# Four stacked attention layers on one core: maxima added to the scores by one product per tile and round, and another sequence of pieces in the second attention

## The reference

```python
# layer 0: 16 heads
x = ln(x + mha(x, x, causal=True));  x = ln(x + mha(x, ctx));  x = ln(x + ffn_gelu(x))
# layer 1: 4 heads
x = x + mha(x, x); x = x + swiglu(x); x = x + mha(x, ctx); x = x + swiglu(x)
# layer 2: 8 heads, beside it a recurrence over the 100 rows
h_t = (1 - gate) * h_prev + gate * z_t + g_t * h_prev     # gate = sigmoid(... + h_prev @ Wgh)
x = x + h_seq + mha(q, ctx) + 0.1 * v;  x = x + ffn_gelu(rms(x))
# layer 3
a = softmax(x @ ctx.T);  x = tanh(concat(x, a @ ctx) @ W + b) + x
```

## Time and profile before

| | |
|---|---|
| median of 3 runs | 1629.91 us (1627.28 to 1635.43) |
| the profiled execution | 1633.46 us, span 1631.7 us |
| TensorE busy | 1569.6 us, 96% |
| VectorE busy | 766.9 us, 47% |
| ScalarE busy | 670.7 us, 41% |
| mean granted TensorE clock | 0.969 |
| products with maxima (L530) | 1152, mean 236 ns |
| score products (L533), in passes | 2304, means 299 and 343 ns |

### The profile page before, as it was taken

The page is one execution under the profiler, slowest core; times in us unless marked ns, Lnnn a source line. Parts: engine busy times, 40 slices in busy tenths (PEclk is TensorE's granted clock), DMA queues, the critical chain, the costliest instruction groups (busy, mean ns, idle before and its releaser), DMA issues.

```text
span 1631.7 us, 30754 instructions
## 1 busy us (share of the span) xinstructions
PE 1569.6 (96%) x13256; PEld 1026.5 (63%) x13256; DVE 766.9 (47%) x1568; ACT 670.7 (41%) x1417; POOL 252.2 (15%) x442
## 2 busy tenths in 40 slices
PE   8899899999999999999999999999899999999997
PEld 7555566666665556555677765554677767665565
DVE  1577657667642256211233332226565567562132
ACT  2455456646554433111333422125453444343343
POOL 1333300100000000000122210000243344320000
PEclk9999999999999999999999999999798799899999
DMA  4311000000000010000100000000000000020031
GB/s 154 99 50 43 12 27 2 1 2 1 2 27 0 0 78 1 20 1 0 78 1 1 1 11 16 0 7 1 27 2 2 2 2 2 2 77 0 0 93 58
DMA packets 19560, 36.97 MB, mean 23 GB/s; under 512 B 2048, under 2 KB 17376, under 8 KB 18272
## 3 DMA queue, kind: packets, MB, share of 16 engines
q1 hardware_dynamic: 19424, 35.01, 6.5%
HBM read 33.36 MB, written 1.64 MB: 21 GB/s over the span
## 4 chain that ended last, share of the span: by engine, by line
PE 87%; DVE 7%; ACT 4%; issue 1%; DMA 1%; POOL 0%; SPq 0%; DVEq 0%; ACTq 0%
PE psum L420 38%; PE psum L755 11%; PE psum L533 9%; PE psum L465 8%; PE psum L571 6%; PE psum L503 3%; PE psum L860 2%; PE psum L530 2%; DVE maxima L1387 2%; PE psum L888 1%; PE psum L901 1%; PE psum L853 1%; PE psum L869 1%; ACT probs L1063 1%; PE psum L566 1%
## 5 line engine op out<-in xcount | busy, mean ns | idle before, releaser
L420 PE MATMUL psum<-x_resid,weights 128*128 128x400 f32 x832 | 294.5, 504 | 4.3 <-ACT probs L1063 1.6
L1387 DVE TENSOR_REDUCE maxima<-psum 100x2 f32<-100x722 f32 (+3 forms) x332 | 243.5, 758 | 113.7 <-PE psum L503 96.1
L420 PEld LDWEIGHTS psum<-x_resid,weights 128*128 128x128 f32 x832 | 156.1, 191 | 121.9 <-issue 5.1
L1063 ACT ACTIVATE probs<-psum 128x800 f32<-128x800 f32 (+3 forms) x240 | 171.6, 748 | 142.8 <-PE psum L533 142.4
L755 PE MATMUL psum<-weights 128*128 128x400 f32 x512 | 174.8, 499 | 0.7 <-DVE maxima L1387 0.7
L420 PE MATMUL psum<-weights,ctx_t 128*128 128x256 f32 (+1 forms) x576 | 162.2, 407 | 0.2 <-ACT values L1034 0.2
L465 PE MATMUL psum<-ctx_t,weights 128*128 128x361 f32 x384 | 144.8, 504 | 1.9 <-DVE weights L1615 0.8
L755 PEld LDWEIGHTS psum<-weights 128*128 128x128 f32 x512 | 97.2, 190 | 75.1 <-DVE maxima L1387 0.8
L530 PE MATMUL psum<-max_rows,ones_bf 32*128 32x200 bf16 (+7 forms) x1152 | 132.0, 236 | 2.3 <-DVE maxima L1387 0.7
L420 PEld LDWEIGHTS psum<-weights,ctx_t 128*128 128x128 f32 (+1 forms) x576 | 101.9, 191 | 39.7 <-issue 13.8
L984 ACT ACTIVATE weights<-psum 128x400 f32<-128x400 f32 (+2 forms) x80 | 38.0, 475 | 209.3 <-PE psum L420 209.3
(11 more groups left out here) (151 smaller groups left out, 2214.2 us busy)
## 6 DMA issues: line engine op xcount, KB each, us to landing
weights<-in_w SPq DMA_DIRECT2D x2, 3072.0 KB, 9.6
staged<-in_ctx SPq DMA_DIRECT2D x32, 128.0 KB, 2.2
values<-in_ctx SPq DMA_DIRECT2D x32, 128.0 KB, 2.1
weights<-in_w SPq DMA_DIRECT2D x3, 1024.0 KB, 4.7
weights<-in_src SPq DMA_DIRECT2D x1, 2368.0 KB, 13.9
weights<-in_w SPq DMA_DIRECT2D x1, 2048.0 KB, 8.8
weights<-in_tw SPq DMA_DIRECT2D x2, 1024.0 KB, 5.8
staged<-in_ctx SPq DMA_DIRECT2D x16, 105.0 KB, 2.2
```

The source lines that it names most:

```text
L420: i = nc.tensor.matmul(PS[0:rows, bk, 0:n], lhs, rhs, start=k == 0, stop=k == len(terms) - 1)
L1063: nc.scalar.activation(PT[0:kn, k % PROBS_KEPT, :, 0:n], PS[0:kn, bk:bk + 2, 0:n], ACT.Exp).then_inc(act_results, mark("act", f"{t} p{b} { ...
L1387: nc.vector.reduce_max(top, src, AX).then_inc(dve_results, mark("dve", f"{t} m{b} {j}"))
```

## The change

A round's maxima are added once per tile: one bf16 product whose moving operand is MB's columns of all the round's c values, each repeated over that c's chunks by a stride of zero, starts the sum of the whole round. The score products follow, and the last one ends the sum. In c0 the sequence of pieces is another. Nothing else differs.

```diff
-    "c0": "T0 T1 P1 n0 R0 R1 R2 n1 V0 T2 R3 T3 F T4 T5 R4 V1 R5 F K0 T6 T7 F K1 V2 p0 X",
+    "c0": "T0 T1 P1 n0 R0 n1 R1 R2 V0 T2 R3 R4 T3 F T4 T5 R5 V1 K0 F T6 T7 K1 V2 F p0 X",
...
+            kn = a["keys"][of[0][1]][1]
+            c0, c1 = of[0][0], of[-1][0] + 1
+            chunks = len(of) // (c1 - c0)
+            for d in range(2):
+                rows = tile_rows(t, i0 + d)
+                maxima = MB[rows, b % 2, c0 * n:c1 * n].rearrange("p (c n) -> p c n", n=n)
+                nc.tensor.matmul(PS[0:kn, bk + d, 0:len(of) * n], ONEB[rows, 0:kn],
+                                 maxima.unsqueeze(2).broadcast_to([a["tile"], c1 - c0, chunks, n]), start=True, stop=False)
             for m, (c, kc) in enumerate(of):
-                k0, kn = a["keys"][kc]
                 for d in range(2):
-                    nc.tensor.matmul(PS[0:kn, bk + d, m * n:(m + 1) * n], ONEB[tile_rows(t, i0 + d), 0:kn],
-                                     MB[tile_rows(t, i0 + d), b % 2, c * n:(c + 1) * n], start=True, stop=False)
-                for d in range(2):
-                    i = nc.tensor.matmul(PS[0:kn, bk + d, m * n:(m + 1) * n], keys_of(t, b, i0 + d, c, k0, kn), queries_of(t, b, i0 + d, c),
-                                         start=False, stop=True)
+                    i = nc.tensor.matmul(PS[0:kn, bk + d, m * n:(m + 1) * n], keys_of(t, b, i0 + d, c, a["keys"][kc][0], kn), queries_of(t, b, i0 + d, c),
+                                         start=False, stop=m == len(of) - 1)
```

## The result

The changed kernel took **1607.7 us** (median of 4 executions, 1605.5 to 1612.1) against 1628.8 for the kernel before: ratio 0.9866, interval 0.9831 to 0.9901. That is 21 us less, outside the predicted range of 1611 to 1633; the forecast of 1622.2 missed two thirds of the gain. The profiled execution took 1612.1 us, with 1610.3 of span.

What follows compares the result with a forecast made beforehand. TensorE, busy 96% of the span, was taken as the bound, except where it waits for VectorE or ScalarE. c1 -2.5, s1 -0.7, c2 -6.5 and c0's order +2.0 made -7.7: 1622.2 us against the median 1629.9, range 1611 to 1633.

Steps and rivals of the forecast that it cites:

- c2 alone: Stage c2: fewer products with maxima shorten its rounds, 0.2 + 0.8 + 4.0 + 1.4, in all -6.5 us.
- The products outside c2: Fewer products with maxima in the other stages: c1 -2.5 us, s1 -0.7, s0 nothing.
- The sequence: Stage c0: the new order of pieces adds waits and costs +2.0 us together.
- the waits it named: c0: T3 waits for T2's maxima until about X + 6.5; the query product behind V2 waits 0.5 to 0.6 us.
- the kinds of item: The four items of a c0 group: 0, +0.65, +0.24 (+0.9 in the last group) and -0.54 us.
- The four-chunk round's 0.21: A round of four chunks saves 0.21 us, with bounds of nothing and 0.36.
- the kept product's 0.17: The one wide product left in a four-chunk round takes 0.17 us for its 400 columns.
- c1's 0.07: c1: the second round waits for its PSUM pair, so only 0.07 of the first round's 0.21 us counts.
- The 1.05 us named as a sign: c1: four-chunk rounds of about 1.05 us would show the forecast right.
- double in three that ran at half clock: c2: round 1 sheds its 0.21 us in 16 items, twice that in three items at half clock.
- rival 3: c0: added waits lower its clock, from 0.99 to 0.90 giving 1644 us; chance 0.08.
- Rival 1: c0 is bound by TensorE and T3's wait is smaller: 1604 us, half-way 1613; chance 0.20 with the half-way case.

Runs made afterwards that it cites:

- products_only: The kernel before with the wide product in all stages, c0's old sequence kept: mean 1612.5 us, ratio 0.9882.
- experiments 3 and 4: Reruns of the changed kernel, and it or the kernel before with more or fewer products with maxima in c2: ratios 0.9861 to 1.0038.
- six over four: The changed kernel with c2's round 1 wide product issued six times, against four times: ratios to the kernel before 0.9927 and 0.9954.
- three over one: before_r1_three compared with before_r1_one: ratios to the kernel before 1.0026 and 1.0038.
- order_only: The kernel before with c0's new sequence and the old products: mean 1626.1 us, ratio 0.9972.
- products_not_c2: The kernel before with the wide product everywhere but in c2, old sequence: mean 1617.9 us, ratio 0.9933.
- products_c2: The kernel before with the wide product in c2 alone, old sequence: mean 1620.9 us, ratio 0.9956.
- c2_wide_twice: The changed kernel with every wide product of c2 issued twice: mean 1617.0 us, ratio 0.9911.
- c2_no_maxima: The changed kernel without any product with maxima in c2: mean 1610.2 us, ratio 0.9870.
- before_r1_three: The kernel before with three wide products added in front of its narrow ones in c2's round 1: mean 1630.5 us, ratio 1.0026.
- before_r1_one: The kernel before with one wide product added in front of its narrow ones in c2's round 1: mean 1637.0 us, ratio 1.0038.

## Why the prediction was wrong

**The arithmetic was right in the main.** The sum was -7.7 us; at an equal clock the change measures -9.7, with about 1 us of error (-10.7 to -8.3 by the rates 12.0 and 15.6). Products: forecast -9.7, measured -9.8. c2 alone: -6.5 against -5.0 by the executions, and 1.5 us per group by the rows (6 for four groups). The products outside c2: -3.2 against -4.7, of which the items of products_only show 1.5 in c0, where the sum had nothing; so that the products' total was met so closely is luck, two misses of 1.5 us that cancel. The sequence: forecast +2.0, measured +0.2 by the executions and +0.9 by the rows; the waits it named came with their releasers, T5's came beside them, and the lengths of the kinds of item were met within 0.2 us each. The four-chunk round's 0.21, the kept product's 0.17 and c1's 0.07 were each met by a row. The 1.05 us named as a sign for c1's first round can't be read there, since the next round waits for its pair.

**The step that failed is the clock.** The sum took every duration at the profile's own clock, carried c2's 0.90 over unchanged and gave no reason ("double in three that ran at half clock" is the only place where the clock enters), and let the clock move in one way only, down, in c0 (rival 3). The range gave it 8 us of scatter. In the runs the mean clock went from 0.9688 to 0.9755 over 22 executions, and to 0.9785 in the first four, which is 13 us of their 21; what is left is 8. So of the missing 13 us, all but one or two lie in the granted clock. Some 4 of these are chance by means, the first four executions having been granted more than the kernel's mean; the median of the 22, 1607.4, is nevertheless close to that of the four.

**Where the clock came from.** By the windows it is c2 behind its first group that ran at full clock in the profile. By experiments 3 and 4 its clock doesn't follow the work: a kernel with less removed, or with work added, gets it as well. That it follows how long a group is fits best, but is argued. For it: the counts by length, and the two pairs with lengths placed beforehand, where the kernel with more work had the higher clock by 0.0066 (six over four) and 0.011 (three over one). Against its being the whole: see what stays open.

Rival 3's mechanism, that waits make the clock fall in c0, did not come: c0 was granted 0.98 after 0.99 with 7.4 us more of waiting (9.8 after 2.4 by the rows above), and order_only, with these waits and the old products, had no lower clock than the kernel before (0.9716 against 0.9688). T3's waits were 0.3 to 0.4 us, shorter than the 0.5 to 1.3 that rival 3 reckoned with, so longer ones stay untested. The Trainium skill, "TensorE: Matmul & The Clock Gate" on PSUM-queue depth-cycling, tells of a kernel whose clock oscillated from short idles between groups of matmuls; the 19 added waits, 0.8 us at most, didn't lower c0's clock here by more than that 0.01. By the same page's Part 3, on what overlaps, a removed product would have returned its weight load as well, an estimate of 0.32 for a four-chunk round. The rows give 0.21, and a wide product added costs 0.17, which is what its 400 columns take by the earlier trace rows; so here the load was hidden.

**Rival 1** (c0 bound by TensorE alone) would have given a time near the measured one, 1604, and for the wrong reason: c0 is 0.8 us shorter, not 14.

What stays open: products_not_c2 has c2 as it was, with groups of 73.0 us, and yet one mid-c2 stretch instead of three and a clock of 0.9740. products_c2 has groups of 71.5 us and a clock of only 0.9716; its profile spent 69 us at half clock outside c2, the most of all (the others 32 to 65), among it two stretches of 10 us in c0, which has no edit. c2_wide_twice and c2_no_maxima have lengths of the worse set and 0.9745 and 0.9740, not clearly below the changed kernel's 0.9755. So where a stage begins, or what goes before it, seems to count as well as the length; no run varied that alone. There is one profile of each kernel, while the mean clocks are of whole executions. Nor is it shown why a group of 71.5 or 75 us meets the places well; that it stands to the moments of change as the group before it did is argued from the lengths alone.

## What to carry to other kernels

Where a stage is granted less than full clock, look in the trace for the places at which the half-clock stretches begin. If they are places of a repeated item and many passes of them go unharmed, the clock is a term of the forecast, with a range of its own both ways, for any edit that changes the item's length: here 0.01 of clock was some 13 us, more than the whole arithmetic of the change. Keep the two apart when reading a result too, by fitting time against granted clock over the executions, or an edit is credited with what the clock gave; and test a suspected rhythm with added work, since a kernel that does more and takes no longer can't be explained by work.

## What the hardware showed unexpectedly

- A kernel with at least 5 us more work took no longer than the one without it, by the granted clock (before_r1_three and before_r1_one: 0.9755 and 0.9645, 1630.5 and 1637.0 us by means, error 3).
- Two stretches with the same busy time of TensorE, 4.05 and 4.06 of 4.80 us, were followed by 0.50 and 1.00 of granted clock.
- Removing three bf16 products of 100 columns and widening the fourth to 400 saved 0.21 us a round, although the columns streamed stayed the same; a product of 400 columns costs 0.17 whether it is added or removed.
